# One query tile's depthwise conv on TensorE in 2x2 phases, the other tile's taps shared by VectorE and GpSimd

## The reference, cut to what matters

```python
qkv = concat([h @ wq.T, h @ wk.T, h @ wv.T])            # 768 channels, 32x32 pixels
dw  = conv_general_dilated(qkv, dw_kernel, (1, 1), 'SAME', feature_group_count=768)   # 5x5, one filter per channel
pw  = conv_general_dilated(dw, pw_kernel, (1, 1), 'VALID', feature_group_count=96)    # 1x1, in groups of 8 channels
qkv_all = concat([qkv, pw])                              # raw heads and convolved heads
# relu linear attention over heads of 8 channels, projection, batch norm, + x
# then: norm, energy = F^T G, softmax over 1024 keys, values, 1x1 output, + input
```

## Time and profile before

| | |
|---|---|
| median of 3 runs | 652.06 us (652.04 to 652.4) |
| the profiled execution's own time | 653.32 us |
| its span (first to last instruction) | 651.5 us |
| mean granted clock of TensorE | 0.995 |
| PE / DVE / POOL / ACT busy | 612.1 / 524.2 / 494.0 / 472.8 us |
| steady period, image 1 to 2 (start of the projection, 137.8 to 285.5) | 147.7 us |

### The profile page before, as it was taken

How to read it: one execution, slowest core, us unless ns; L and a number is a source line. 1 busy time by engine, 2 the same in 40 slices (tenths; PEclk the granted TensorE clock), 3 DMA queues, 4 the chain that set the end, 5 groups by cost and what they waited for, 6 DMA issues and landing times.

```text
span 651.5 us, 13132 instructions
## 1 busy us (share of the span) xinstructions
PE 612.1 (94%) x5448; PEld 442.6 (68%) x5448; DVE 524.2 (80%) x616; ACT 472.8 (73%) x772; POOL 494.0 (76%) x236
## 2 busy tenths in 40 slices
PE   4997999989899999999899999999899999899997
PEld 3864366646678887556578886556568875376897
DVE  4899899777899799977899999969889995274543
ACT  4697679888686798988687897997688685244331
POOL 4859949967999999959999999989999996013000
PEclk9999899999999999999999999999999999999999
DMA  8000000101100000001200000000100000000000
GB/s 319 3 10 5 1 3 3 65 2 64 65 2 17 16 18 19 1 2 64 66 1 17 16 18 18 3 1 1 64 1 18 16 19 18 0 1 1 16 17 33
DMA packets 6698, 16.67 MB, mean 26 GB/s; under 512 B 880, under 2 KB 1136, under 8 KB 6128
## 3 DMA queue, kind: packets, MB, share of 16 engines
q1 hardware_dynamic: 6640, 15.84, 6.8%
HBM read 11.64 MB, written 4.19 MB: 24 GB/s over the span
## 4 chain that ended last, share of the span: by engine, by line
PE 80%; DVE 8%; ACT 6%; POOL 2%; issue 2%; DMA 1%; SPq 0%; POOLq 0%; DVEq 0%; ACTq 0%
PE ps L762 14%; PE ps L786 13%; PE ps L878 7%; PE ps L597 4%; PE ps L531 4%; PE ps L777 4%; PE ps L535 4%; PE ps L532 4%; PE ps L810 3%; PE ps L844 2%; DVE ps L1371 2%; PE ps L635 2%; ACT prod L1071 2%; PE ps L697 2%; PE ps L580 2%
## 5 line engine op out<-in xcount | busy, mean ns | idle before, releaser
L1639 POOL TENSOR_TENSOR conv<-conv,prod 128x930 f32<-128x930 f32 (+4 forms) x174 | 381.8, 2236 | 35.0 <-ACT prod L1071 32.0
L1371 DVE SCALAR_TENSOR_TENSOR ps<-raw,dw_sb,ps 128x930 f32<-128x930 f32 (+4 forms) x264 | 317.3, 1202 | 6.8
L1071 ACT ACTIVATE prod<-raw,dw_sb 128x961 f32<-128x961 f32 (+4 forms) x209 | 217.8, 1109 | 5.3 <-POOL conv L1639 3.9
L786 PE MATMUL ps<-ht,pt 128*128 128x256 f32 x384 | 87.4, 381 | 0.0
L786 PEld LDWEIGHTS ps<-ht,pt 128*128 128x128 f32 x384 | 71.1, 190 | 11.5 <-issue 2.5
L1239 ACT ACTIVATE rows<-ps,small 128x1024 f32<-128x1024 f32 x32 | 35.6, 1114 | 58.7 <-DVE small L1560 58.4
L1639 POOL TENSOR_TENSOR rows<-rows,prod 128x930 f32<-128x930 f32 (+4 forms) x26 | 58.2, 2239 | 11.7 <-ACT prod L1071 8.1
L1555 DVE TENSOR_REDUCE small<-ps 128x1 f32<-128x1024 f32 x32 | 39.1, 1222 | 20.5 <-PE ps L762 20.5
L762 PE MATMUL ps<-hi,t_hi 128*128 128x512 f32 x128 | 43.9, 424 | 8.1 <-DVE t_lo L1543 5.3
L762 PE MATMUL ps<-lo,t_hi 128*128 128x512 f32 x128 | 39.9, 392 | 0.0
L531 PE MATMUL ps<-hi,wqkv_hi 128*128 128x512 f32 x92 | 37.8, 411 | 0.0
(11 more groups left out here) (185 smaller groups left out, 1168.3 us busy)
## 6 DMA issues: line engine op xcount, KB each, us to landing
q_raw<-x_dram SPq DMA_DIRECT2D x8, 512.0 KB, 5.6
x<-x_dram SPq DMA_DIRECT2D x4, 1024.0 KB, 4.7
out_dram<-x_t SPq DMA_DIRECT2D x16, 256.0 KB, 2.0
conv<-wqkv_dram SPq DMA_DIRECT2D x1, 768.0 KB, 4.2
conv<-fg_dram SPq DMA_DIRECT2D x1, 512.0 KB, 6.1
proj_sb<-proj_dram SPq DMA_DIRECT2D x1, 512.0 KB, 7.7
pw_sb<-pw_dram SPq DMA_DIRECT2D x1, 384.0 KB, 6.9
mask_sb<-masks_dram SPq DMA_DIRECT2D x1, 280.0 KB, 6.2
```

The costliest lines, as they stand in the source:

```text
L786: mm = pe.matmul(dst[:, 0:C], pt[:, i % PT_BUFS, j, :], ht[:, j, :], start=(j == 0), stop=(j == NB - 1))
L1071: act.activation(dst, view, ACT.Copy, scale=weight(t, i)).then_inc(prod_ready, 1)
L1371: return dve.scalar_tensor_tensor(dst, view, w, before, ALU.mult, ALU.add)
L1639: pool.tensor_tensor(total, total, product, ALU.add).then_inc(conv_pool, 1)
```

## The change

Tile 0's whole conv goes to PE, in another form. Its image is split into four phases (even and odd rows, even and odd columns) of 16x16 pixels with a border, 18x18. A block of 32 rows of the weights holds 8 channels times 4 phases in, 8 channels times 4 phases out, so one matmul does all taps that fall on one of nine offsets of the phases: 9 offsets x 4 blocks of 8x4 channels x 4 groups, 144 matmuls of 32x32 weights with 256 columns, no diagonal. ACT writes the phases while it copies the raw queries out of PSUM (`stage`, two copies of 256 elements for one of 512). Sixteen DMAs from SBUF to SBUF bring the phases from `stage` to `phased`, where channels and phases share partitions. The weights (`tap_weights`) are loaded from DRAM for each image, since `phased` and `tap_weights` lie in the memory of `t_hi` and `t_lo`, which the softmax attention uses. `phase_conv(b + 1)` stands in the middle of image b, after the second output weights; ACT copies its four banks out (`phase_sums`, 256 columns each). The 1x1 conv of tile 0 is then 16 matmuls of 128x32 weights and 256 columns.

All small-tile taps of tiles 0 and 1 are gone, with their weights, their copies and `whole` in the queries; tile 5 of image 0 keeps its own. Tile 1 has no taps on PE: 8 late taps on POOL (9 in image 0), 17 on DVE (16). DVE has 67 taps an image for 75 (66 for 63 in image 0), POOL 48 own and 7 late adds for 50 and 9. The tables are new, all of this shape:

```diff
-LATE_OF = (9, 10, 10, 10)
-SHARED_OF = (0, 3, 3, 3)
-QUAD_OF = (16, 12, 12, 12)
+LATE_OF = (9, 8, 8, 8)
+SHARED_OF = (0, 0, 0, 0)
...
-LATES_PWKV = ((1, 0, 0, 0, 0, 0, 0, 5), (0, 0, 0, 0, 0, 0, 0, 3), (0, 0, 0, 0, 0, 0, 0, 2), (0, 0, 0, 0, 0, 0, 0, 1))
+LATES_PWKV = ((2, 0, 1, 0, 0, 0, 0, 5), (0, 0, 0, 0, 0, 0, 0, 2), (0, 0, 0, 0, 0, 0, 0, 4), (1, 0, 0, 0, 0, 0, 0, 0))
...
+            def load_phases(b):
+                sp.wait_ge(a_free, A_RQ[b][2 * PHASE_TILE + 1] + 1)
+                for f in range(PHASES):
+                    for g in range(QUADS):
+                        sp.dma_start(phased[f::PHASES, g, :], stage[g::QUADS, f, :]).then_inc(phases_loaded, 16)
...
-            def shared_quads(b, h):
-
-                pe.wait_ge(a_free, A_RQ[b][-1] + 1)
-                pe.wait_ge(quad_weights_ready, b + 1)
-                quads(A_AT[f"sums_{h}", b], SHARED_TILE, h, QUAD_SEQ[b], later_weights if b else first_weights[SHARED_TILE])
+            def phase_conv(b):
+
+                pe.wait_ge(taps_loaded, 16 * (b + 1))
+                pe.wait_ge(phases_loaded, 16 * PHASES * QUADS * (b + 1))
+                for e, (ey, ex) in enumerate(OFFSETS):
+                    for r in range(QUADS):
+                        k = slice(r * QUAD, (r + 1) * QUAD)
+                        bank = a_slot(A_AT["sums", b] + r) if e == 0 else a_bank(A_AT["sums", b] + r)
+                        for g in range(QUADS):
+                            view = phased_img[k, g, 1 + ey:PSIDE - 1 + ey, 1 + ex:PSIDE - 1 + ex]
+                            mm = pe.matmul(bank[g * QUAD:(g + 1) * QUAD, 0:QUARTER], tap_weights[k, e, g, :], view,
+                                           start=(e == 0), stop=(e == len(OFFSETS) - 1))
+                mm.then_inc(a_full, QUADS)
...
+                    for x in range(2):
+                        for r in range(QUADS):
+                            mm = pe.matmul(dst[r * QUAD:(r + 1) * QUAD, x * QUARTER:(x + 1) * QUARTER],
+                                           pw_ph[:, r, 2 * h + x, :], conv_ph[:, r, :], start=True, stop=True)
...
+                    for y in range(2):
+                        mm = act.copy(stage_img[:, 2 * y:2 * y + 2, rows_at, 1:PSIDE - 1],
+                                      src.rearrange("p (a y c x) -> p y x a c", y=2, c=SIDE // 2, x=2)[:, y])
...
+            def phase_sums(b):
+
+                slot = A_AT["sums", b]
+                act.wait_ge(a_full, slot + QUADS)
+                for r in range(QUADS):
+                    act.copy(conv_ph[:, r, :], a_bank(slot + r)[:, 0:QUARTER]).then_inc(a_free, 1)
...
-                if with_next:
-                    pe.wait_ge(exp_done, NB * (b + 1))
-                    shared_quads(b + 1, 0)
...
-            for t in first_weights:
-                op = quad_products(dve, first_weights[t], t, NTAPS)
-            op.then_inc(quad_weights_ready, 1)
+            dve.tensor_tensor(first_weights, quad_ident.unsqueeze(1).to_broadcast([P, NTAPS, QUAD]),
+                              dw_sb[:, FIRST_TILE, :].unsqueeze(2).to_broadcast([P, NTAPS, QUAD]),
+                              ALU.mult).then_inc(quad_weights_ready, 1)
...
-                    pool.wait_ge(d_full, D_AT["proj", b] + D_PROJ)
-                    quad_products(pool, later_weights, SHARED_TILE, QUAD_OF[b + 1]).then_inc(quad_weights_ready, 1)
```

More of the change, by code:

```diff
@@ L501, in _ @@
             for b in range(B):
+                if b + 1 < B:
+                    if b == 0:
+                        sp.wait_ge(a_full, A_AT["sums", 0] + QUADS)
+                    load_taps()
+                    load_phases(b + 1)
                 if b + 2 < B:
@@ L619, in first_whole @@
                 whole(dst, lambda r: quad_ident, h, True).then_inc(a_full, 1)
-            def shared_quads(b, h):
-                pe.wait_ge(a_free, A_RQ[b][-1] + 1)
-                pe.wait_ge(quad_weights_ready, b + 1)
-                quads(A_AT[f"sums_{h}", b], SHARED_TILE, h, QUAD_SEQ[b], later_weights if b else first_weights[SHARED_TILE])
-            def queries(b, t, h):
-                dst, cols, late = a_slot(A_AT["pwq", b] + 2 * t + h), slice(h * HALF, (h + 1) * HALF), t == SHARED_TILE
-                own = any(tap[0] == t for tap in DVE_SEQ[b] + POOL_SEQ[b])
-                last = [tap for tap in DVE_SEQ[b] if tap[0] == t][-1:]
-                if h == 0 and last:
-                    pe.wait_ge(conv_dve, dve_count(b, DVE_SEQ[b].index(last[0]) + 1))
-                if own:
-                    mm = pe.matmul(dst, pw_sb[:, t, :], conv[:, t, cols], start=True, stop=(b > 0 and not late))
-                if late and LATE_SEQ[b]:
-                    if h == 0:
-                        pe.wait_ge(conv_pool, late_add_count(b, late_adds_of(b)))
-                    pe.matmul(dst, pw_sb[:, t, :], late_of[b][:, cols], start=not own, stop=False)
-                if late or b == 0:
-                    if h == 0 and not late:
-                        pe.wait_ge(pw_quads_loaded, 16)
-                    pe.wait_ge(a_free, (A_AT[f"sums_{h}", b] if late else A_AT[f"first_{2 + h}", b]) + QUADS)
-                    mm = whole(dst, lambda r: pw_quad[:, t, r, :], h + (2 if late and b == 0 else 0),
-                               not own and not (late and LATE_SEQ[b]))
@@ L843, in body @@
                         if t < 2 * CK:
-                            pe.matmul(dst[:, c0:c0 + P], block, pw_sb[:, t, :], start=True, stop=True)
+                            pe.matmul(dst[:, c0:c0 + P], block, pw_sb[:, 2 * CK + t - 1, :], start=True, stop=True)
                         else:
@@ L1219, in body @@
                     fused_weights(A_AT["mb_raw", b + 1], 0)
+                    phase_sums(b + 1)
                 x1_transposes(b, 3)
@@ L1387, in conv_taps @@
                     before = None if starts else acc
-                    if t == SHARED_TILE and starts and SHARED_OF[b]:
-                        before = final
-                        dve.wait_ge(conv_pool, add_count(b, len(ADD_SEQ[b])))
                     tap(final if i == NTAPS - 1 else acc, t, i, before).then_inc(conv_dve, 1)
@@ L1714 @@
     pw_bd[:, 2 * CK:] = pw_bd[:, 2 * CK:].transpose(2, 1, 0).copy()
-    pw_quads = np.stack([pw_bd[r:r + QUAD, :CK, r:r + QUAD] for r in range(0, P, QUAD)], 2)
-    pw_quads = np.tile(pw_quads, (QUADS, 1, 1, 1)).reshape(P, CK, P)
+    group, unit, ch = np.meshgrid(np.arange(QUADS), np.arange(QUADS), np.arange(D), indexing="ij")
+    channel = QUAD * unit + QUADS * ch + group
+    pw_phases = np.zeros((P, QUADS, PHASES, QUAD), pw.dtype)
+    taps_phases = np.zeros((P, len(OFFSETS), QUADS, QUAD), dw.dtype)
+    for t in (PHASE_TILE,):
+        for f in range(PHASES):
+            for co in range(QUAD):
+                pw_phases[QUAD * group + D * f + ch, unit, f, co] = pw_bd[channel, t, QUAD * unit + co]
+            for to in range(PHASES):
+                for e, (ey, ex) in enumerate(OFFSETS):
+                    dy, dx = 2 * ey + f // 2 - to // 2 + PAD, 2 * ex + f % 2 - to % 2 + PAD
+                    if 0 <= dy < TAPS and 0 <= dx < TAPS:
+                        taps_phases[QUAD * unit + PHASES * ch + f, e, group, D * to + ch] = dw[t * P + channel, TAPS * dy + dx]
     head_rows = np.tile(np.kron(np.eye(HEADS), np.ones((1, D))), (QUARTERS, 1))
```

192 lines of the change are left out of this document (105 added, 87 removed).

## The result

The changed kernel takes 650.1 us (median of six runs, 648.95 to 650.91), the kernel before took 652.5 in the same session: 0.9941 of it, 95% interval 0.9916 to 0.9965. It is faster by 0.6% or some 2.4 us; the prediction was 641.8, with a range from 633 to 650. The profiled execution has a span of 649.1 (time 650.91), against 651.5 (653.32) before.

The account below looks back on a forecast made before the run. PE was taken to bound the kernel, with POOL, DVE and PE all near in image 0. -8.3 + 5.5 + 0.7 = -2.1 us an image, -6.3 for three, and -4.0 for image 0 took 652.06 to 641.8 us; range 633 to 650.

Parts of the forecast that it names:

- What was removed: Later images on PE: small-tile units 3.4 and 3.2 us, queries 1.7 less; 8.3 us an image gained.
- The phase conv: Added on PE in later images: nine waves of 0.55 us plus 0.5 to drain, 5.5 us.
- Rival 2: Phase conv's waves keep an extra of 0.25 to 0.34 us: conv 7.1 us, time 646.6; chance 0.13.
- The first wave of a unit: Profile row used to size the conv: 16 tiles start within 0.11 us, so a wave takes 0.55.
- The two small waits: PE at the phase conv: its fourth bank, and transposes behind it needing ACT's first copy; 0.7 us for both.
- The fold behind it moves along as it is: Behind the phase conv: the fold, where PE waits 0.70 for `fold_lo`, was to shift unchanged.
- Image 0: Up to the end of image 0's queries, POOL, DVE and PE all near: -4.0 us, bounds -1 and -7.
- Hidden work: Off the path, an image: 9.6 us less DVE taps, 8.9 POOL adds, 5.5 ACT products; gives only slack.

Follow-up runs that it names:

- the fastest kernel: Changed kernel with the conv in two pieces, fold's spread and eight output weights between, eight behind, ACT's products and DVE's taps moved: 638.9 us, ratio 0.977.
- the longer stand-in: Changed kernel with 64 dense matmul instructions an image in place of the phase conv of images 1 to 3: 667.2 us.

## Why the prediction was wrong, step by step

- *What was removed* was right: 8.3 us an image forecast, 8.6, 9.4 and 9.0 measured, with the wait for ACT's last key/value copy at 0.74 to 0.9 where 0.8 stood (244.48 in the first later image). 0.6 of the 9.4 is a pause of the kernel before (399.02, at nothing that the profile shows) that did not come again.
- *The phase conv* was mis-sized. Taken were 0.55 a wave and 5.5 us; it took 0.71 a wave, and 6.9, 6.7 and 6.5 us with a pause of 0.3 to 0.5 that I had not thought of. The first wave of a unit was the wrong row to lean on: 16 starts in 0.11 us do not tell how soon the next wave may follow. Rival 2, the waves with an extra of 0.25 to 0.34, had the size. The page "TensorE: Matmul & The Clock Gate" of the Trainium skill, section "Back-to-back issue gap", which stood beside it, gives about 25 ns from start to start at the least, for few columns; here 288 instructions took 22 ns each, and 15 ns at half the columns, so that floor is not what paces small tiles side by side.
- *The two small waits* were 0.55 instead of 0.7: ACT's copy, as said, and nothing for the fourth bank.
- *"The fold behind it moves along as it is"* is the step that failed. It ignored that the change had moved DVE's taps in the same place, and it assumed full clock behind the conv. In the second and third image DVE alone sets the length: from the conv's start to the denominators it is 16.9 and 15.5 us, and with one offset of nine, a conv of 1.05 us, it is 17.8 and 15.5. So there a conv of the forecast's 5.5 us would have gained nothing either. In the first image DVE is through with its taps at 157.1, before the conv ends, and the loss is the conv's size and the clock. So 6.2 us an image became 8.1, 10.2 and 8.7.
- *The clock* was in no step and in no rival. Of the three stretches of about 3.4 us at half speed behind the convs the first cost 0.7, the second about 0.9 (an estimate: `fold_lo` is done at 313.8, and from there to the denominators the kernel before takes 2.05 us, not 2.95), and the third nothing, since DVE was later; the fourth, at the end, cost 1.7.
- *Image 0* was right: 3.6 of 4.0 us. PE was ready for the late matmul at 110.55, where 110.7 was forecast, and POOL's late adds ended at 111.2, where 109 to 110 was, so that POOL still set the time, by 0.76. 2.0 more came from the pause in the scores that went away; no step had it, and it is luck.
- *Hidden work* was right: POOL's busy time fell by 7.7 and 13.9 us (9 to 10 forecast for each period, 10.8 on average), PE waited for POOL once, 0.8 us in image 0, and never before a conv for its DMAs.

By the forecast's own steps the sum is then, for what was gained, -5.6 for image 0 and -26.9 for three images, and for what was lost, +27.0 at the conv, +2.2 at the end and 0.9 of small differences: -2.4, as measured. That most of the loss was not the conv's own, the fastest kernel shows: with the same conv and the same arithmetic it takes 638.9 us, 3 us less than the forecast.

## What to carry to other kernels

When work is put into the bound engine's stream, read what the other engines have queued at that place, and price the first thing that each of them will be late with; a table that was written for another order of work is part of the change. Look for work that is already there to lie between and behind pieces of a light stretch, rather than for a place for it in one piece; and when one engine is made faster at a place, move the others' work in the same edit: here DVE's taps alone, moved in one period, gave nothing, the two pieces without ACT's products lost 4 to 9 us, and all three gained 11.

## What the runs showed of the hardware

- PE's clock fell to 0.50, its 1.2 GHz level, behind stretches with waits of only 0.3 to 0.6 us, without any long idle time: behind the first and the third conv of the changed kernel (a pause of 0.51 and 0.31, then a wait of 0.55). Behind its second conv a wait of 1.80 came on top. With DVE's taps moved it fell behind one conv of three, the one with the longest pause (0.39 against 0.22 and 0.12), and for 7 to 10 us when the conv had half its columns and pauses of 1.3 to 1.6. In the fastest kernel, where dense matmuls lie between the two pieces of the conv and behind them, it did not fall behind any of the three later convs. The Trainium skill, page "TensorE: Matmul & The Clock Gate", section "A second HAM failure mode: psum-queue depth-cycling", tells of a clock that swings because the engine idles often and briefly between groups; the traces agree as to short waits. Dense matmuls in the conv's place, with the same wait of 0.55 behind and no pause, kept the clock up in two of three images and lost it in the one with a wait of 1.51. Where exactly it tips, and whether small tiles count by themselves, was not settled. Nor was the fall at 564: the wait of 1.48 there stands in every kernel of this study, and the clock stayed up behind it in the kernel before, with the longer stand-in and in the fastest kernel.
- The pauses of PE at nothing that the profile shows, those ahead of an instruction that waits for no semaphore, go with the loading of its own instructions. The 13 traces, of both kernels and the eleven runs, hold PE's instructions (matmuls, weight loads and separate waits) in order, and the 16 KB packets of the queue that the profile's page calls `instruction` (packets, MB, and their time as a share of the 16 DMA engines' span):

```profile
q8 instruction: 44, 0.72, 0.5%
```

  Counted from the program's start, every pause of 0.08 us or more, 44 in all, stands within two instructions of one place in a grid of 256. Between two such places PE took 1.3 to 3.05 us, without the pause, wherever it paused, and 3.19 us or more at the other 497 places, where it did not. Ahead of each pause one packet landed 1.2 to 1.6 us before PE went on. So the conv in one piece always stops at the same matmul (behind its 202nd, 199th or 195th), and the pause varies with the packet: 0.51 and 0.22 us at the same place, where the packet took 1.33 and 0.88 us. In two pieces the same place lies in the second piece; the 256 instructions ahead of it, with longer matmuls among them, took 4.5 to 4.9 us, and PE did not stop. The pause of 2.12 in the scores of the kernel before was such a place too, and went away when the change shifted these places to others of PE's instructions. The Trainium skill, page "Advanced Engine Details and Errata", section "ISA Cache", has instructions come in lines of 256, of which only two are held; the traces agree with the 256, and show nothing of how many lines are held.
